# First attention of a gated cross-attention network: the row maxima read from a pair of PSUM banks and a single one

## The chip, the cores and the metric

One Trainium2 chip, one of its cores. The time is the device time of one execution in microseconds (us). Before the change it was 6643.13 us, the median of three runs (6642.96 to 6648.73).

## What is computed

Two layers of gated cross-attention and feed-forward on x of 8 x 256 tokens with 256 features, against a context of 8 x 1601 tokens. The change lies in the attention of the first layer. There the batch is flattened: 2,048 queries meet all 12,808 keys, in 16 heads of 16 features. Queries, keys and values are rounded to 8 bits (fake quantisation), and so are the attention weights, per query:

```
attn = softmax(q @ k.T)                        # (16, 2048, 12808)
s    = max(max(attn, axis=-1) / 255, 1e-8)
attn = clip(round(attn / s), 0, 255) * s
out  = attn @ v
```

Dividing by the row's maximum means that exp(score - max + ln 255) is the number to be rounded, so the kernel needs each query's largest score over all keys before it can take the first exponential of that query.

## The kernel before, in words

`first_attention` works in 32 passes: 16 heads, and for each two chunks of 1,024 queries (`QC`). A pass has `NE` = 102 tiles of 126 keys. `IB` = 4 passes form the body of a loop that runs `LOOPS` = 8 times (the first body is written out before it).

Two computations of the same scores run side by side.

The first is for the exponentials. For tile s PE multiplies keys by queries in two halves of 512 queries (`e_half`, line 1047) into one of two pairs of PSUM banks (banks 0 to 3), with keys on the partitions. ACT takes the exponential of the 126 x 1024 tile into `a_e` (line 1151), POOL rounds it by adding and storing as fp16 in `a_p` (line 918), and PE, four tiles later (`LAG`), multiplies by the values (`av`, line 1087) and adds up the unrounded part for the row sums (line 1091) in bank 4. The scores for exponentials use rows 0 to 53 of PE's array.

The second is for the maxima, one pass ahead. Queries are on the partitions here, and the scores come in `NM` = 201 pieces: 8 tiles of 128 queries x 25 blocks of 512 keys, and one last piece with the 8 keys that are left for each of the 8 query tiles. A piece is one matmul of 512 columns (line 1064) into one of three banks (5, 6, 7), taken in turn (`SLOTS` = 3), and one VectorE reduction by maximum (line 1180) into a column of `a_mx`. These matmuls use rows 64 to 111 of the array. PE waits before piece j until the reduction of piece j - 3 has been counted in `max_done` (line 1062); VectorE waits for `scores_m`. When all 201 pieces of a pass are there, `maximum` reduces the columns (line 1191), and POOL, after rounding tile 93 of the running pass (`SPLIT`), splits the result into three bf16 parts (lines 900 to 910), PE transposes them after tile 98 (`TURN`, line 1073), and ACT copies them into the queries (line 1136), where the next pass's exponentials need them from their tile 0 on.

PE's program is one list, `order`, written before the engines' programs: a half of the scores for exponentials, then a piece of the maxima, then the second half, then a piece, then the values of the tile four back. A pass has 204 such slots for 201 pieces, so three slots are without a piece. The pieces of a pass are rotated: `AHEAD` = 20 of them are made at the end of the pass two before it is used. Waits stand where they are written, and what follows a wait on PE waits with it.

Before the first pass there is an opening: all 201 pieces of pass 0, with nothing else on PE, and then the first `AHEAD` of pass 1.

The DMA queue (SP) loads keys, queries and values of later passes at counts of finished exponentials; its waits do not use the maxima.

Of the kernel before, what the change touches and what calls it, by code (L numbers as in the profile page):

```python
# [9 lines left out]
ALU = mybir.AluOpType  # L10
ACT = mybir.ActivationFunctionType
AX = mybir.AxisListType
# [30 lines left out]
class Shapes:  # L43


    def __init__(self, x_shape, ctx_shape):
        self.B, self.LQ, _ = x_shape
        self.LK = ctx_shape[1]
        self.T = self.B * self.LQ
        self.NT = self.T // P  # L50
        self.NK = self.B * self.LK

        self.QC = 1024
        self.QT = self.QC // P
        self.NC = self.T // self.QC
        self.KT = 126
        self.KTILES = (self.NK + self.KT - 1) // self.KT
        self.NE = self.KTILES
        self.KLAST = self.NK - (self.KTILES - 1) * self.KT
        assert 0 < self.KLAST <= self.KT and self.KTILES % 2 == 0  # L60

        self.SLOTS = 3
        self.WHOLE = self.NK // BANK
        self.LEFT = self.NK - self.WHOLE * BANK
        self.PIECES = [(((t, c * BANK, BANK, 0),), t * (self.WHOLE + 1) + c) for t in range(self.QT) for c in range(self.WHOLE)]
        self.PIECES.append((tuple((t, self.WHOLE * BANK, self.LEFT, t * self.LEFT) for t in range(self.QT)), None))
        self.NM = len(self.PIECES)
        assert 0 < self.LEFT and self.QT * self.LEFT <= BANK and self.NM % self.SLOTS == 0
        self.VQ = (self.KTILES + 3) // 4

        self.KT1 = (self.LK + P - 1) // P
        self.K1LAST = self.LK - (self.KT1 - 1) * P
# [13 lines left out]
class Kernel:  # L86
# [705 lines left out]
    def first_attention(self):  # L792


        nc, sh = self.nc, self.sh
        NE, NM, NC, KT, QC, QT, PIECES = sh.NE, sh.NM, sh.NC, sh.KT, sh.QC, sh.QT, sh.PIECES
        IB = 2 * NC
        LOOPS = HEADS // 2
        RE = 8
        LAG = 4  # L800
        AHEAD = 20
        TURN = NE - 4
        SPLIT = NE - 9
        QW = QC // 4
        V_DMAS = 4
        assert IB == 4 and (IB * NE) % RE == 0 and NE % 2 == 0 and (RE - LAG) >= 2
        LN255 = math.log(255.0)
        K_DMAS, Q_DMAS, O_DMAS = 9, 6, 8
        with ExitStack() as ctx:
# [7 lines left out]
            p = self.sb(ctx, "a_p", [P, RE, QC], F16)  # L817
            sel = self.sb(ctx, "a_sel", [P, 2 * HD])
            mx = self.sb(ctx, "a_mx", [P, QT * (sh.WHOLE + 1)])
# [13 lines left out]
            av_done, scores_m, max_done = (self.sem(ctx, n) for n in ("av_done", "scores_m", "max_done"))  # L833
# [14 lines left out]
            O_BANK, M_BANK = 4, 5  # L848

            def key_rows(t):  # L850
                return sh.KLAST if t == sh.KTILES - 1 else KT

            stream = [("m", 1, j) for j in range(AHEAD, NM)] + [("m", 2, j) for j in range(AHEAD)]
            order, owed = [], []
# [19 lines left out]
            def _(g):  # L876
# [9 lines left out]
                def held(sem, value):  # L886
                    g.wait_ge(sem, value)
                    g.sem_inc(pool_held, 1)

                def split(it, ii, first=False):  # L890

                    n, hb, t0 = it * IB + ii, (ii // NC) % 2, (ii % NC) * QT
                    c = n * LINKS
# [19 lines left out]
                def body(it, i):  # L913
                    for s in range(NE):
                        kk = i * NE + s
                        rows = key_rows(s)
                        held(exp_done, it * (IB * NE) + kk + 1)
                        g.tensor_scalar(p[0:rows, kk % RE, :], e[0:rows, kk % RE, :], 1.0, SHIFT,  # L918
                                        ALU.mult, ALU.add).then_inc(rounded, 1)
                        if s == SPLIT:  # L920
                            held(rounded, it * (IB * NE) + kk + 1)
                            split(it, i + 1)
                split(0, 0, True)
                for i in range(IB):
                    body(0, i)
                with g.Fori(1, LOOPS) as it:
                    for i in range(IB):
                        body(it, i)
# [9 lines left out]
            def load_inv(sp, h, b):  # L938
                sp.dma_start(Kb[M_AT:M_AT + IROWS, b, :], self.d_inv[h]).then_inc(ld_k[b], 16)

            def load_v(sp, h, b, at):
                r = slice(at * P // V_DMAS, (at + 1) * P // V_DMAS)
                sp.dma_start(Vb[r, b, :, :].rearrange("p t d -> p (t d)"), self.d_v0[h, r, 0:sh.KTILES * 2 * HD]).then_inc(ld_v[b], 16)
# [15 lines left out]
            def _(sp):  # L959
# [12 lines left out]
                sp.sem_inc(ld_k[0], 16 * 3)  # L972
                for at in range(V_DMAS):
                    load_v(sp, 0, 0, at)
# [8 lines left out]
                def body(g, i, first):  # L983
# [20 lines left out]
                    if i % NC == 0:  # L1004
# [7 lines left out]
                        load_inv(sp, h, b)  # L1012
                        for at in range(V_DMAS):
                            sp.wait_ge(exp_done, n * NE + 56 + 8 * at)
# [17 lines left out]
                for b in range(2):  # L1032
                    sp.wait_ge(ld_k[b], 16 * K_DMAS * (LOOPS + (b == 0)))
                    sp.wait_ge(ld_v[b], 16 * V_DMAS * (LOOPS + (b == 0)))

            @block.tensor
            def _(pe):
# [14 lines left out]
                def m_piece(g, i, ahead, j, first=False):  # L1052

                    n, ii = g * IB + i + ahead, i + ahead
                    if j == 0:
                        pe.wait_ge(ld_q[ii % 4], 16 * Q_DMAS * (g + ii // 4 + 1))
                        if ii % NC == 0 and not first:
                            pe.wait_ge(ld_k[(ii // NC) % 2], 16 * K_DMAS * (g + ii // NC // 2 + 1))
                    if first and j in range(0, sh.WHOLE, sh.WHOLE // FIRST):
                        pe.wait_ge(ld_first[j // (sh.WHOLE // FIRST)], FIRST_LOADED[j // (sh.WHOLE // FIRST)])  # L1060
                    if not (first and j < sh.SLOTS):
                        pe.wait_ge(max_done, n * NM + j + 1 - sh.SLOTS)
                    for t, k0, wd, c0 in PIECES[j][0]:
                        last = pe.matmul(self.PS[:, M_BANK + j % sh.SLOTS, c0:c0 + wd], Qb[M_ROWS, ii % 4, t * P:(t + 1) * P],  # L1064
                                         Kb[M_ROWS, (ii // NC) % 2, k0:k0 + wd], start=True, stop=True)
                    last.then_inc(scores_m, 1)

                def m_turn(g, i, bank):
                    pe.wait_ge(m_split, g * IB + i + 2)
# [7 lines left out]
                def av(g, i, t, first_ever):  # L1077
# [3 lines left out]
                    if t == 0:  # L1081
                        if not first_ever:
                            pe.wait_ge(gathered, n)
                        if i % NC == 0:
                            pe.wait_ge(ld_v[i // NC], 16 * V_DMAS * (g + 1))
                    for j in range(4):
# [27 lines left out]
                m_turn(0, -1, 2)  # L1114
                for j in range(AHEAD):
                    m_piece(0, 0, 1, j)
# [55 lines left out]

            @block.vector
            def _(v):
                def m_piece(n, j):
                    v.wait_ge(scores_m, n * NM + j + 1)
                    _, col = PIECES[j]
                    bank = self.PS[:, M_BANK + j % sh.SLOTS, :]
                    if col is not None:
                        v.tensor_reduce(mx[:, col:col + 1], bank, AX.X, ALU.max).then_inc(max_done, 1)  # L1180
                    else:
                        dst = mx[:, :].rearrange("p (t c) -> p t c", t=QT)[:, :, sh.WHOLE]
                        v.tensor_reduce(dst, bank[:, 0:QT * sh.LEFT].rearrange("p (t c) -> p t c", t=QT), AX.X,
                                        ALU.max).then_inc(max_done, 1)

                def maximum(n, first):

                    v.wait_ge(max_done, (n + 1) * NM)
                    if not first:
                        v.wait_ge(m_split, n)  # L1190
                    v.tensor_reduce(ms[:, 0, :], mx[:, :].rearrange("p (t c) -> p t c", t=QT), AX.X,
                                    ALU.max).then_inc(m_ready, 1)
                    v.wait_ge(m_ready, n + 1)

                def body(g, i):
                    for j in range(AHEAD, NM):
                        m_piece(g * IB + i + 1, j)
                    maximum(g * IB + i + 1, False)
                    for j in range(AHEAD):
                        m_piece(g * IB + i + 2, j)  # L1200

                for j in range(NM):
                    m_piece(0, j)
                maximum(0, True)
                for j in range(AHEAD):
                    m_piece(1, j)
                for i in range(IB):
                    body(0, i)
                with v.Fori(1, LOOPS) as g:
                    for i in range(IB):  # L1210
                        body(g, i)
# [657 lines left out]
    def second_attention(self):  # L1869
# [11 lines left out]
        SLOTS = 3  # L1881
        AHEAD = 12
        TURN = NE - 2
# [579 lines left out]
```

## Time and profile before

| | |
|---|---|
| median of 3 runs | 6643.13 us |
| profiled execution, its own time | 6652.62 us |
| its span in the profile | 6650.8 us |
| first attention after its opening | 720 to 4900 us |
| PE busy over the span | 5788.3 us (87%) |
| DVE busy | 5609.7 us (84%) |
| ACT busy | 4504.5 us (68%) |
| POOL busy | 3781.9 us (57%) |

PE is TensorE's matmuls and PEld its weight loads, DVE is VectorE, ACT ScalarE, POOL GpSimd, SP the engine that issues the DMAs. Busy time of an engine is the union of its instructions; a group's mean is the length of one instruction, from start to end, and these overlap by a little, so that the distance from start to start is shorter. "Idle before" with an arrow gives the time for which the engine had nothing to do just before such instructions, and whose semaphore ended it. The granted clock is a share of TensorE's full 2.4 GHz; 0.5 is 1.2 GHz. Ends of matmuls are modelled.

### The profile page before, as it was taken

How to read it: one execution, taken by the hardware profiler on the slowest of the kernel's cores; microseconds unless marked ns; L12 is line 12 of the kernel's file. 1: busy time of each engine (PE TensorE's matmuls, PEld its weight loads, DVE VectorE, ACT ScalarE, POOL GpSimd, SP SyncE). 2: the span in 40 equal slices, each digit the busy share in tenths (PEclk: the TensorE clock that was granted, in tenths of full speed). 3: DMA queues.
4: the chain of work that ended last, by engine and by line, in shares of the span. 5: the costliest groups of instructions: out<-in, count | busy, mean ns of one | idle time of the engine just before them, and what ended most of it. 6: DMA issues, size and time to landing. Idle time of an engine off the chain costs nothing. (4 is left out here: it accounts for less than half of the span.)

```text
span 6650.8 us, 180101 instructions
## 1 busy us (share of the span) xinstructions
PE 5788.3 (87%) x64160; PEld 2456.0 (37%) x64160; DVE 5609.7 (84%) x8987; ACT 4504.5 (68%) x4373; POOL 3781.9 (57%) x4001
## 2 busy tenths in 40 slices
PE   2865999999999999999999999999978577999824
PEld 2651233333333333333333333333344353544412
DVE  4877999999999899899989999989963646777786
ACT  0650598898898889888989988988842012666512
POOL 2330488888788788788878878878840001000021
PEclk7995799999999999999999999999989787999966
DMA  1544101101101001011011010010110068777700
GB/s 58 131 115 126 18 9 23 21 8 27 18 11 25 15 16 25 7 24 21 8 27 18 11 25 15 16 23 9 22 37 0 10 267 222 114 110 111 112 28 11
DMA packets 176565, 315.50 MB, mean 47 GB/s; under 512 B 91731, under 2 KB 137812, under 8 KB 171042
## 3 DMA queue, kind: packets, MB, share of 16 engines
q1 hardware_dynamic: 175656, 303.45, 21.3%
q8 instruction: 561, 9.19, 0.6%
q14 instruction: 348, 2.85, 0.2%
HBM read 192.39 MB, written 113.07 MB: 46 GB/s over the span
## 5 line engine op out<-in xcount | busy, mean ns | idle before, releaser
L1180 DVE TENSOR_REDUCE a_mx<-PS 128x1 f32<-128x512 f32 x6620 | 4073.1, 686 | 240.3 <-PE PS L1064 236.7
L1151 ACT ACTIVATE a_e<-PS,a_sk 126x1024 f32<-126x1024 f32 x3264 | 3634.0, 1114 | 494.5 <-PE PS L1047 146.0
L918 POOL TENSOR_SCALAR a_p<-a_e 126x1024 f16<-126x1024 f32 x3264 | 3413.4, 1046 | 681.7 <-ACT a_e L1151 628.6
L1047 PE MATMUL PS<-a_Q,a_K 54*126 54x512 bf16 x6528 | 2112.3, 404 | 31.9 <-issue 22.7
L1064 PE MATMUL PS<-a_K,a_Q 48*128 48x512 bf16 (+1 forms) x6884 | 2108.7, 383 | 31.1 <-POOL a_p L883 30.8
L1091 PE MATMUL PS<-a_e,a_sel 126*32 126x256 f32 x26112 | 1996.2, 382 | 28.1 <-issue 28.1
L1047 PEld LDWEIGHTS PS<-a_Q,a_K 54*126 54x126 bf16 x6528 | 615.3, 131 | 1383.8 <-issue 1325.1
L1087 PE MATMUL PS<-a_p,a_V 128*32 128x256 f16 x13056 | 960.4, 284 | 14.3 <-ACT a_og L1132 10.3
L1087 PEld LDWEIGHTS PS<-a_p,a_V 128*32 128x32 f16 x13056 | 336.8, 93 | 1251.5 <-POOL a_p L918 1053.5
L1091 PEld LDWEIGHTS PS<-a_e,a_sel 126*32 126x32 f32 x26112 | 756.4, 110 | 38.3 <-issue 32.0
L2137 DVE TENSOR_REDUCE b_mx<-PS 128x1 f32<-128x512 f32 x803 | 504.6, 685 | 188.1 <-PE PS L2021 188.0
L2111 ACT ACTIVATE b_e<-PS 128x1024 f32<-128x1024 f32 (+1 forms) x416 | 415.7, 1024 | 223.6 <-PE PS L2041 220.9
L1064 PEld LDWEIGHTS PS<-a_K,a_Q 48*128 48x128 bf16 x6884 | 404.3, 94 | 167.0 <-DVE a_mx L1180 129.4
L2187 POOL TENSOR_SCALAR b_ms<-b_ms 128x8 f32<-128x8 f32 x33 | 7.7, 233 | 631.0 <-DVE b_ms L2148 631.0
L2021 PE MATMUL PS<-b_K,b_Q 96*128 96x512 bf16 (+1 forms) x1070 | 279.8, 346 | 50.1 <-POOL b_K L2172 41.1
L2041 PE MATMUL PS<-b_Q,b_K 99*128 99x256 bf16 (+1 forms) x1664 | 256.0, 277 | 15.4 <-ACT b_e L2111 9.5
L486 PE MATMUL PS<-wkv,cT 128*126 128x256 f32 (+1 forms) x816 | 207.5, 386 | 47.7 <-DVEq L551 47.7
L2056 PE MATMUL PS<-b_e,b_V 128*32 128x256 f32 (+1 forms) x3328 | 229.1, 388 | 9.0 <-ACT b_og L2096 6.6
L1807 POOL MEMSET v1v<- 128x6656 f32 x2 | 11.2, 5646 | 378.8 <-POOLq L1734 378.8
L1846 ACT ACTIVATE k1f<-PS,bk 128x512 f32<-128x512 f32 x64 | 36.3, 593 | 269.5 <-PE PS L1821 269.5
L2041 PEld LDWEIGHTS PS<-b_Q,b_K 99*128 99x128 bf16 (+1 forms) x1664 | 142.2, 99 | 162.2 <-ACT b_e L2111 79.1
L1136 ACT ACTIVATE a_Q<-PS 6x1024 bf16<-6x1024 bf16 x33 | 33.5, 1016 | 242.0 <-PE PS L1073 241.2
(321 smaller groups left out, 3522.1 us busy)
## 6 DMA issues: line engine op xcount, KB each, us to landing
b_K<-d_k SPq DMA_DIRECT2D x210, 200.1 KB, 6.3
a_K<-d_k SPq DMA_DIRECT2D x99, 400.2 KB
d_v<-v1v SPq DMA_DIRECT2D x9, 3328.0 KB, 10.3
b_V<-d_v SPq DMA_DIRECT2D x36, 832.0 KB, 12.4
d_k<-k_T SPq DMA_DIRECT2D x100, 252.0 KB, 4.0
d_k<-k1p SPq DMA_DIRECT2D x54, 400.2 KB, 6.9
a_V<-d_v SPq DMA_DIRECT2D x68, 204.0 KB, 2.8
d_v<-vq SPq DMA_DIRECT2D x17, 803.2 KB
```

The lines of the kernel that those rows point to most:

```text
L918: g.tensor_scalar(p[0:rows, kk % RE, :], e[0:rows, kk % RE, :], 1.0, SHIFT, ALU.mult, ALU.add).then_inc(rounded, 1)
L1047: last = pe.matmul(self.PS[0:key_rows(s), e_bank(i, s) + y, :], Kb[0:E_ROWS, (i // NC) % 2, s * KT:s * KT + key_rows(s)], Qb[0:E_ROWS, i % ...
L1064: last = pe.matmul(self.PS[:, M_BANK + j % sh.SLOTS, c0:c0 + wd], Qb[M_ROWS, ii % 4, t * P:(t + 1) * P], Kb[M_ROWS, (ii // NC) % 2, k0:k0 ...
L1087: pe.matmul(self.PS[32 * j:32 * j + 32, O_BANK, 0:QW], Vb[:, i // NC, t, :], p[:, kk % RE, j * QW:(j + 1) * QW], start=(t == 0), stop=Fals ...
L1091: last = pe.matmul(self.PS[32 * j:32 * j + 32, O_BANK, 0:QW], sel[0:key_rows(t), :], e[0:key_rows(t), kk % RE, j * QW:(j + 1) * QW], start ...
L1151: a.activation(e[0:r, kk % RE, :], self.PS[0:r, e_bank(i, s):e_bank(i, s) + 2, :], ACT.Exp, scale=skb[0:r, hb, s:s + 1]).then_inc(exp_done, 1)
L1180: v.tensor_reduce(mx[:, col:col + 1], bank, AX.X, ALU.max).then_inc(max_done, 1)
L2021: last = pe.matmul(self.PS[:, M_BANK + j % SLOTS, c0:c0 + wd], Qb[0:ROWS, ii % SETS, tq * P:(tq + 1) * P], Kb[0:ROWS, ii % SETS, hh, k0:k0 ...
L2041: last = pe.matmul(self.PS[0:rows, e_bank(s) + j // 2, (j % 2) * LQ:(j % 2 + 1) * LQ], Kb[0:ROWS + MROWS, i % SETS, j, s * P:s * P + rows] ...
L2056: last = pe.matmul(self.PS[32 * j:32 * j + 32, O_BANK, 0:LQ], Vb[0:rows, i // 4, s, i % 4 * QH + j, :], e[0:rows, k % RE, j * LQ:(j + 1) * ...
L2111: a.activation(e[0:r, kk % RE, :], self.PS[0:r, e_bank(s):e_bank(s) + 2, :].rearrange("p b n -> p (b n)"), ACT.Exp).then_inc(exp_done, 1)
L2137: v.tensor_reduce(mx[:, col:col + 1], bank, AX.X, ALU.max).then_inc(max_done, 1)
```

## The change

The three banks are used as a pair and a single one. Pieces 3k and 3k + 1 go to banks 5 and 6, and one reduction reads both (128 x 1024 elements, two results); piece 3k + 2 goes to bank 7 and is reduced alone, as before. A pass then has `NG` = 134 reductions in place of 201. `max_done` and `scores_m` count these groups. PE waits before the first piece of a pair until the pair before has been reduced, before a single piece until the single one before has been, and not at all before the second piece of a pair. It signals VectorE after the second piece of a pair and after a single one. `AHEAD` becomes 21, so that the rotation falls between triples.

```diff
--- before.py
+++ after.py
@@ -66,6 +66,8 @@
         self.PIECES.append((tuple((t, self.WHOLE * BANK, self.LEFT, t * self.LEFT) for t in range(self.QT)), None))
         self.NM = len(self.PIECES)
         assert 0 < self.LEFT and self.QT * self.LEFT <= BANK and self.NM % self.SLOTS == 0
+        self.NG = 2 * (self.NM // self.SLOTS)
+        assert self.SLOTS == 3
         self.VQ = (self.KTILES + 3) // 4
 
         self.KT1 = (self.LK + P - 1) // P
@@ -794,15 +796,18 @@
 
         nc, sh = self.nc, self.sh
         NE, NM, NC, KT, QC, QT, PIECES = sh.NE, sh.NM, sh.NC, sh.KT, sh.QC, sh.QT, sh.PIECES
+        NG = sh.NG
         IB = 2 * NC
         LOOPS = HEADS // 2
         RE = 8
         LAG = 4
-        AHEAD = 20
+        AHEAD = 21
         TURN = NE - 4
         SPLIT = NE - 9
         QW = QC // 4
         V_DMAS = 4
+        group_of = lambda j: 2 * (j // 3) + (j % 3 == 2)
+        assert AHEAD % 3 == 0
         assert IB == 4 and (IB * NE) % RE == 0 and NE % 2 == 0 and (RE - LAG) >= 2
         LN255 = math.log(255.0)
         K_DMAS, Q_DMAS, O_DMAS = 9, 6, 8
@@ -1058,12 +1063,13 @@
                             pe.wait_ge(ld_k[(ii // NC) % 2], 16 * K_DMAS * (g + ii // NC // 2 + 1))
                     if first and j in range(0, sh.WHOLE, sh.WHOLE // FIRST):
                         pe.wait_ge(ld_first[j // (sh.WHOLE // FIRST)], FIRST_LOADED[j // (sh.WHOLE // FIRST)])
-                    if not (first and j < sh.SLOTS):
-                        pe.wait_ge(max_done, n * NM + j + 1 - sh.SLOTS)
+                    if j % 3 != 1 and not (first and j < sh.SLOTS):
+                        pe.wait_ge(max_done, n * NG + group_of(j) - 1)
                     for t, k0, wd, c0 in PIECES[j][0]:
                         last = pe.matmul(self.PS[:, M_BANK + j % sh.SLOTS, c0:c0 + wd], Qb[M_ROWS, ii % 4, t * P:(t + 1) * P],
                                          Kb[M_ROWS, (ii // NC) % 2, k0:k0 + wd], start=True, stop=True)
-                    last.then_inc(scores_m, 1)
+                    if j % 3 != 0:
+                        last.then_inc(scores_m, 1)
 
                 def m_turn(g, i, bank):
                     pe.wait_ge(m_split, g * IB + i + 2)
@@ -1172,20 +1178,28 @@
 
             @block.vector
             def _(v):
-                def m_piece(n, j):
-                    v.wait_ge(scores_m, n * NM + j + 1)
+                def m_group(n, j):
+
+                    v.wait_ge(scores_m, n * NG + group_of(j) + 1)
                     _, col = PIECES[j]
-                    bank = self.PS[:, M_BANK + j % sh.SLOTS, :]
-                    if col is not None:
-                        v.tensor_reduce(mx[:, col:col + 1], bank, AX.X, ALU.max).then_inc(max_done, 1)
+                    if j % 3 == 0:
+                        c1 = PIECES[j + 1][1]
+                        v.tensor_reduce(mx[:, col:c1 + 1:c1 - col], self.PS[:, M_BANK:M_BANK + 2, :], AX.X, ALU.max).then_inc(max_done, 1)
+                    elif col is not None:
+                        v.tensor_reduce(mx[:, col:col + 1], self.PS[:, M_BANK + 2, :], AX.X, ALU.max).then_inc(max_done, 1)
                     else:
                         dst = mx[:, :].rearrange("p (t c) -> p t c", t=QT)[:, :, sh.WHOLE]
-                        v.tensor_reduce(dst, bank[:, 0:QT * sh.LEFT].rearrange("p (t c) -> p t c", t=QT), AX.X,
+                        v.tensor_reduce(dst, self.PS[:, M_BANK + 2, 0:QT * sh.LEFT].rearrange("p (t c) -> p t c", t=QT), AX.X,
                                         ALU.max).then_inc(max_done, 1)
 
+                def m_groups(n, j0, j1):
+                    for j in range(j0, j1):
+                        if j % 3 != 1:
+                            m_group(n, j)
+
                 def maximum(n, first):
 
-                    v.wait_ge(max_done, (n + 1) * NM)
+                    v.wait_ge(max_done, (n + 1) * NG)
                     if not first:
                         v.wait_ge(m_split, n)
                     v.tensor_reduce(ms[:, 0, :], mx[:, :].rearrange("p (t c) -> p t c", t=QT), AX.X,
@@ -1193,17 +1207,13 @@
                     v.wait_ge(m_ready, n + 1)
 
                 def body(g, i):
-                    for j in range(AHEAD, NM):
-                        m_piece(g * IB + i + 1, j)
+                    m_groups(g * IB + i + 1, AHEAD, NM)
                     maximum(g * IB + i + 1, False)
-                    for j in range(AHEAD):
-                        m_piece(g * IB + i + 2, j)
-
-                for j in range(NM):
-                    m_piece(0, j)
+                    m_groups(g * IB + i + 2, 0, AHEAD)
+
+                m_groups(0, 0, NM)
                 maximum(0, True)
-                for j in range(AHEAD):
-                    m_piece(1, j)
+                m_groups(1, 0, AHEAD)
                 for i in range(IB):
                     body(0, i)
                 with v.Fori(1, LOOPS) as g:
```

## Rows read from the trace of the kernel before

**Rows 1.** The page's costliest groups: busy us, mean ns, idle before, releaser.

```profile
L1180 DVE TENSOR_REDUCE a_mx<-PS 128x1 f32<-128x512 f32 x6620 | 4073.1, 686 | 240.3 <-PE PS L1064 236.7
L1151 ACT ACTIVATE a_e<-PS,a_sk 126x1024 f32<-126x1024 f32 x3264 | 3634.0, 1114 | 494.5 <-PE PS L1047 146.0
```

**Rows 2.** Windows: length, busy us of PE, PEld, DVE, ACT, POOL; clock, DMA.

```profile
720.00:4900.00 4180.00, 4106.50 (x52593) 1457.88 (x52592) 3972.42 (x6484) 3673.42 (x3329) 3451.98 (x3454) 0.98 0.09 18
1400.00:1500.00 100.00, 100.00 (x1308) 35.43 (x1296) 98.01 (x161) 90.98 (x82) 84.41 (x86) 1.00 0.01 2
620.00:716.00 96.00, 95.23 (x167) 16.22 (x166) 96.00 (x162) 0.00 (x0) 0.00 (x0) 0.50 0.06 12
5700.00:5800.00 100.00, 96.32 (x958) 50.40 (x952) 78.38 (x138) 68.66 (x73) 5.57 (x25) 1.00 0.82 119
```

**Rows 3.** Timeline in the middle of a pass: start, length, engine.

```profile
2506.81 0.43 PE L1047 MATMUL PS<-a_Q,a_K 54*126 54x512 bf16 x1
2506.82 0.39 PE L1064 MATMUL PS<-a_K,a_Q 48*128 48x512 bf16 x1
...
2508.04 0.43 PE L1047 MATMUL PS<-a_Q,a_K 54*126 54x512 bf16 x1
...
2508.05 0.60 PE L1064 MATMUL PS<-a_K,a_Q 48*128 48x512 bf16 x2
...
2508.51 1.29 DVE L1180 TENSOR_REDUCE a_mx<-PS 128x1 f32<-128x512 f32 x2 [0.54 <-PE PS L1064]
2508.61 0.10 PEld L1087 LDWEIGHTS PS<-a_p,a_V 128*32 128x32 f16 x4 [0.39 <-POOL a_p L918]
...
2509.27 0.43 PE L1047 MATMUL PS<-a_Q,a_K 54*126 54x512 bf16 x1
```

**Rows 4.** Timeline of DVE in one pass and at its boundary.

```profile
2466.75 41.23 DVE L1180 TENSOR_REDUCE a_mx<-PS 128x1 f32<-128x512 f32 x67 [0.54 <-PE PS L1064]
...
2546.49 0.69 DVE L1180 TENSOR_REDUCE a_mx<-PS 128x1 f32<-128x512 f32 x1 [0.43 <-PE PS L1064]
2547.51 3.13 DVE L1180 TENSOR_REDUCE a_mx<-PS 128x1 f32<-128x512 f32 x5 [0.33 <-PE PS L1064]
2551.18 8.60 DVE L1180 TENSOR_REDUCE a_mx<-PS 128x1 f32<-128x512 f32 x14 [0.54 <-PE PS L1064]
```

**Rows 5.** Timeline of the opening, before any exponential: DVE and PE's loads.

```profile
679.45 10.84 DVE L1180 TENSOR_REDUCE a_mx<-PS 128x1 f32<-128x512 f32 x18
...
680.05 0.68 DVE L1180 TENSOR_REDUCE a_mx<-PS 128x1 f32<-128x512 f32 x1
...
680.78 0.10 PEld L1064 LDWEIGHTS PS<-a_K,a_Q 48*128 48x128 bf16 x1 [0.49 <-DVE a_mx L1180]
```

**Rows 6.** Groups by line from 720 to 4900 us: idle time and its releaser.

```profile
L1180 DVE TENSOR_REDUCE a_mx<-PS 128x1 f32<-128x512 f32 x6420 | 3953.4, 686 | 209.6 <-PE PS L1064 206.0
L1151 ACT ACTIVATE a_e<-PS,a_sk 126x1024 f32<-126x1024 f32 x3232 | 3598.5, 1114 | 491.4 <-PE PS L1047 146.0
L918 POOL TENSOR_SCALAR a_p<-a_e 126x1024 f16<-126x1024 f32 x3231 | 3379.0, 1046 | 679.1 <-ACT a_e L1151 628.6 <-POOL a_mparts L910 11.0
...
L1064 PEld LDWEIGHTS PS<-a_K,a_Q 48*128 48x128 bf16 x6676 | 383.9, 94 | 37.0 <-DVE a_mx L1180 32.8 <-issue 0.5
```

**Rows 7.** DVE's groups that take 1,024 elements, later in the program.

```profile
L2375 DVE SCALAR_TENSOR_TENSOR gt<-PS,fst,gb 128x1024 f32<-128x1024 f32 x16 | 20.5, 1284 | 28.6 <-PE PS L2314 28.6
L2385 DVE TENSOR_REDUCE gs<-gt 128x1 f32<-128x1024 f32 x16 | 19.5, 1220 | 0.6
```

**Rows 8.** Timeline of a tile at the lower clock.

```profile
1766.88 0.68 PE L1047 MATMUL PS<-a_Q,a_K 54*126 54x512 bf16 x1
...
1766.88 1.03 PE L1064 MATMUL PS<-a_K,a_Q 48*128 48x512 bf16 x2
...
1767.60 1.29 DVE L1180 TENSOR_REDUCE a_mx<-PS 128x1 f32<-128x512 f32 x2 [6.03 <-PE PS L1064]
...
1769.10 0.69 PE L1047 MATMUL PS<-a_Q,a_K 54*126 54x512 bf16 x1
```

## The prediction

> **What bounds the kernel now.** I read the page's groups first. The maxima are the costliest group, 6,620 reductions of 512 scores, and 3,264 exponentials say how many tiles there are: 32 passes of 102 [rows 1]. The windows come next. From 720 to 4900 us, the first attention after its opening, PE is busy 98% of the time and DVE 95% at a mean granted clock of 0.98; at 1400 to 1500 us they are at 100% and 98% [rows 2]. Two engines look full, so the shares don't decide. The timeline does. Tiles follow each other every 1.23 us on PE (2506.81, 2508.04, 2509.27), and PE's part needs no wait: scores from 2508.04, V products from 2508.61 (0.57 later), the next scores 0.66 after that [rows 3]. At 2506.82 a tile has one score block for the maxima in place of two, and it takes the same 1.23 us. DVE, left without a block there, idles 0.54 us, released by PE, and restarts at 2508.51 with no backlog [rows 3]. Between two such holes it makes 67 reductions in 41.23 us, (41.23 - 0.68)/66 = 0.614 us apart, just PE's pace of half a tile [rows 4]. At the opening, where nothing but DVE sets the pace, they stand (10.84 - 0.68)/17 = 0.598 apart [rows 5]. So PE sets the tile and DVE follows, with 2 x (0.614 - 0.598) = 0.03 us per tile to spare. In the whole stage PE's loads waited for DVE 32.8 us in sum; DVE waited for PE 206.0 us [rows 6].
>
> **The change, part by part.** Pieces come in triples. Of three reductions two become one over 1,024 elements. What a long one takes: 1.22 us for a reduction of 1,024 from SBUF, and 1.28 us for another operation that reads 1,024 from PSUM [rows 7]. One of 512 from PSUM takes 0.68 [rows 5]. I take 1.22, which is the same operation; 1.28 is kept as the upper end, and 0.68, no dearer than a short one, belongs to a rival below. DVE's starts then fall from 3 x 0.598 = 1.79 to (1.22 - 0.08) + 0.598 = 1.74 us per triple: 0.05 us that nobody waits for.
>
> The other part is the buffering, and it costs. Before, PE may write a piece as soon as the one three back is read: up to two are in hand while DVE reads. Now the first piece of a pair waits until the whole pair before it has been read, and DVE starts the pair when its second piece is written. The pair's two banks are filled or read, never both; only the single bank works beside them. The wait stands in PE's program before the late scores, the V products and the next tile, so all of these queue behind it.
>
> One turn of the pair, in steps:
> - filling it when both pieces lie in one tile: 0.60 us for two [rows 3];
> - filling it when it straddles two tiles: the piece that waited ends 0.39 after the wait opens (one block, 2506.82). V products start 0.04 before such an end (2508.61 against 2508.05 + 0.60), so at 0.35; the next tile's scores 0.66 later, and their block 0.39 more: 1.40 us [rows 3];
> - to DVE's start: 2508.51 - (2508.05 + 0.39) = 0.07 us [rows 3];
> - the read: 1.22 us [rows 7];
> - back to PE: a reduction that starts at 680.05 ends at 680.73, and the load that waits for it starts at 680.78: 0.05 us [rows 5].
>
> Turns are 0.60 + 1.34 = 1.94 and 1.40 + 1.34 = 2.74 us. A triple is a tile and a half, so the two kinds alternate; both make 4.68 us for three tiles that now take 3.69: 0.99 us more. The tile goes from 1.23 to 1.56 us on average. A pass has 67 triples, 33.5 couples x 0.99 = 33.2 us. Off this I take 1.5 us: the three slots without a piece and PE's own pauses around the pass boundary (DVE idles there 0.43, 0.33, 0.54 us [rows 4]) let a pair drain unseen. 32 passes x 31.7 = 1,014 us.
>
> Two corrections. With the clock at 1.2 GHz a tile already takes 2.22 us (1766.88 to 1769.10) and two blocks 1.03 [rows 8]; a pair's turn is then 1.03 + 1.34 = 2.37 us, and it hides in the tile and a half of 3.3. A mean of 0.98 [rows 2] puts (1 - 0.98)/(1 - 0.50) = 4% of the stage at that clock, 167 us; I count 130 us of it, the rest being pauses, as 60 tiles that lose nothing: 60 x 0.33 = -20 us. At the opening, 620 to 716 us, the clock is 0.50 [rows 2], only these blocks run, and DVE's own three reads make a triple 1.79 us. The pair's turn of 2.37 replaces it: 74 triples (67, and 7 of the next pass) x 0.58 = +43 us.
>
> The rest moves nothing. One wait less per triple on PE and one increment less are in no gap of the trace. AHEAD of 21 for 20 keeps a triple whole and brings the last piece of a pass one slot, 0.6 us, earlier. The softmax chain behind the maximum (the splitting on POOL at tile 93, the transposes) gets five slower tiles to hide in, so it brings no loss. ACT (1.11 of 1.23 us) and POOL (1.05) [rows 6] have more time per tile than now. SP's loads hang on the tiles' count and come later with them. The second attention isn't touched.
>
> **Sum.** 1,014 - 20 + 43 = +1,037 us on the profiled execution, 6652.6 us by itself (span 6650.8 and 1.8 around it). This stands 9.5 us above the median of 6643.1, so I predict 6643 + 1,037, rounded to 7,680 us.
>
> **Two rules beside the rows.** The Trainium skill, Perfetto Trace Analysis, section "Optimizing Scalar/DVE Operations", says that larger operations can improve throughput if the engine is saturated, and also that an engine which isn't saturated but leaves bubbles on others may do better with its instructions broken up. By the first the kernel would gain the 0.05 us per triple; by the second it loses. DVE's 0.54 us idle without a backlog makes the second the one that applies here, and no run here has shown its size.
>
> **Rivals.**
> *DVE is the bound, the kernel gets faster.* For it: DVE is busy 98% at 1400 us [rows 2], and its 0.614 per piece is near its 0.598. If the shared idle were an artefact, the pace would be the reductions', and 33 passes x 67 x 0.05 to 0.06 = 110 to 135 us would go: 6,520 us. It decides where filling the pair and both hand-overs fit into the single read beside it: 0.60 us against 0.60 + 0.12 and 1.40 + 0.12. Neither fits. Chance 0.03.
> *A read of two banks takes hardly longer than one.* Were it 0.68 us, the turns would be 1.40 and 2.20, in sum 3.60 under 3.69, and the tile would stay at PE's 1.23: 6,645 us. Against it stand the rows of 1.22 and 1.28 us for 1,024 elements [rows 7]. It decides below some 0.73 us. Chance 0.04.
> *The clock falls.* PE now stands still for 0.3 of each 1.56 us. In this stage the lower clock comes with long pauses (6.03 us at DVE before the tiles of [rows 8]), and at 620 to 716 us it stays there although a block is issued every 0.60 us [rows 2]; at 5700 to 5800 PE has small pauses and the clock is 1.00 [rows 2]. If it stayed at 1.2 GHz, tiles would take 2.22 us [rows 8]: 3,264 x 0.99 = +3,230, or 9,870 us; if it did so a third of the time, near 8,400. PE would still do most of its present work per us, far more than at the opening, and this is what I hold against it. Chance 0.08.
> The Trainium skill has such a rule: TensorE: Matmul & The Clock Gate, section "A second HAM failure mode: psum-queue depth-cycling", tells of a kernel whose micro-idles between groups of matmuls made the clock swing between its two levels. No row of this trace shows it for pauses as short as these.
>
> **How the numbers follow.** Forecast 0.85. Its own range: hand-over of 0.04 in place of 0.07, more turns absorbed, or part of the late scores overlapping the wait takes off up to 230 us; reading at 1.28 adds 2 x 0.06 x 33.5 x 32 = 129 us, and some passes at the lower clock add up to 150 more. That gives 7,450 to 7,950, and the rivals, all outside it, with what these bounds may miss leave some 2 in 10 out. This kernel's measurements tell 0.2% (13 us) from no change. Faster: 0.03. Within 0.2%: 0.04. Slower: 0.93, the forecast, the clock and what lies between.
>
> **What would show it.** Right: tiles alternating between 1.23 us and about 1.7 us with a mean near 1.56; PE's loads at the maxima's line waiting for DVE in about two tiles of three, and some 1,000 us of such waits in sum where there were 32.8; reductions of 2 x 512 at 1.22 us; DVE's share falling to some 75 to 80%; the clock still near 0.98. Wrong: tiles of 1.23 us with DVE as idle as before (the pair fits after all), a pair read far from 1.22, or a granted clock well under 0.9 in the stage.

## The result, and the profile after

The changed kernel takes 7607.8 us (median of 4 runs, 7600.64 to 7615.57) against 6645.9 us of the kernel before in the same comparison: a ratio of 1.1447, 95% interval 1.1427 to 1.1466, +962 us. The forecast was 7,680 us in a range of 7,450 to 7,950. The profiled execution took 7600.6 us, with a span of 7598.8 us.

In the changed kernel's rows L1052 is the scores for the exponentials, L1069 the blocks for the maxima, L1093 and L1097 the products with the values and the row sums, L1157 the exponential, L1187 the wide reduction and L1189 the single one. The page's groups, with the columns of [rows 1]:

```profile
L1157 ACT ACTIVATE a_e<-PS,a_sk 126x1024 f32<-126x1024 f32 x3264 | 3633.9, 1114 | 1403.5 <-PE PS L1052 1388.8
...
L1187 DVE TENSOR_REDUCE a_mx<-PS 128x2 f32<-128x1024 f32 x2218 | 2717.4, 1225 | 1198.4 <-PE PS L1069 1097.0
...
L1189 DVE TENSOR_REDUCE a_mx<-PS 128x1 f32<-128x512 f32 x2185 | 1488.3, 681 | 43.3 <-PE PS L1069 43.3
...
L1069 PEld LDWEIGHTS PS<-a_K,a_Q 48*128 48x128 bf16 x6885 | 464.7, 94 | 1161.0 <-DVE a_mx L1187 1076.6
```

Two reductions in three have become one of 1,225 ns. DVE is idle 1,097 us before the wide ones, released by PE, and the loads of the blocks for the maxima (PEld) are idle 1,077 us, released by the wide reduction. Each waits for the other in turn. These are sums over the whole execution, opening included; before the change they were 237 us [rows 1] and, for the loads, 129 us. In the passes alone, from 760 to 5800 us:

```profile
L1187 DVE TENSOR_REDUCE a_mx<-PS 128x2 f32<-128x1024 f32 x2127 | 2606.0, 1225 | 1116.3 <-PE PS L1069 1015.9
...
L1069 PEld LDWEIGHTS PS<-a_K,a_Q 48*128 48x128 bf16 x6599 | 443.9, 94 | 980.0 <-DVE a_mx L1187 959.4 <-DVE a_mx L1189 13.9 <-issue 1.8
```

That is 1,016 and 959 us, where [rows 6] had 206 and 33. ACT's work is unchanged at 3,634 us, and its idle time before it has gone from 494 us [rows 1] to 1,404.

The windows, with the columns of [rows 2]:

```profile
720.00:5900.00 5180.00, 4884.98 (x52798) 1641.54 (x52798) 3970.62 (x4393) 3682.47 (x3333) 3460.37 (x3462) 0.99 0.08 15
1400.00:1500.00 100.00, 95.59 (x1046) 31.84 (x1043) 77.08 (x86) 73.42 (x67) 69.14 (x67) 1.00 0.19 31
620.00:716.00 96.00, 59.48 (x123) 9.22 (x121) 74.31 (x83) 0.00 (x0) 0.00 (x0) 0.50 0.06 12
```

The engine that looked nearly full (95% and 98%) is now at 77%, and PE at 94 to 96%. PE still reads as busy because a matmul's span is longer than the distance to the next (0.38 us, and 0.60 for two in a row), and these spans bridge most of a pause: its share does not show that it stands still. The clock is at 0.99, no lower than before.

The timeline in the middle of a pass shows the turns. Columns as in [rows 3].

```profile
3101.17 0.09 PEld L1069 LDWEIGHTS PS<-a_K,a_Q 48*128 48x128 bf16 x1 [0.55 <-DVE a_mx L1187]
...
3101.49 0.10 PEld L1093 LDWEIGHTS PS<-a_p,a_V 128*32 128x32 f16 x4 [0.23 <-issue]
...
3102.15 0.60 PE L1069 MATMUL PS<-a_K,a_Q 48*128 48x512 bf16 x2
...
3102.62 1.23 DVE L1187 TENSOR_REDUCE a_mx<-PS 128x2 f32<-128x1024 f32 x1 [0.90 <-PE PS L1069]
3102.72 0.10 PEld L1093 LDWEIGHTS PS<-a_p,a_V 128*32 128x32 f16 x4 [0.39 <-issue]
...
3103.38 0.43 PE L1052 MATMUL PS<-a_Q,a_K 54*126 54x512 bf16 x1
...
3103.90 0.09 PEld L1069 LDWEIGHTS PS<-a_K,a_Q 48*128 48x128 bf16 x1 [0.40 <-DVE a_mx L1187]
...
3104.13 0.38 PE L1069 MATMUL PS<-a_K,a_Q 48*128 48x512 bf16 x1
...
3104.54 1.23 DVE L1187 TENSOR_REDUCE a_mx<-PS 128x2 f32<-128x1024 f32 x1
...
3105.09 0.43 PE L1052 MATMUL PS<-a_Q,a_K 54*126 54x512 bf16 x1
...
3105.82 0.09 PEld L1069 LDWEIGHTS PS<-a_K,a_Q 48*128 48x128 bf16 x1 [0.55 <-DVE a_mx L1187]
```

At 3101.17 the wait for the pair opens, in the second half of a tile; the V products follow at 3101.49, the next tile's blocks at 3102.15, and the wide read starts at 3102.62. It ends at 3103.85, and at 3103.90 the loads for the next pair start: this turn took 2.73 us. That next pair lies in one tile: its blocks at 3103.90 and 3104.13, the read at 3104.54 (ending 3105.77), the next loads at 3105.82, a turn of 1.92 us. The first half of the scores (3103.38, 3105.09) goes out before the wait; the second half, the V products and the next tile stand behind it.

A pass is the distance between two reductions of all maxima's columns (line 1191 before, 1205 after). Before:

```profile
2537.09 0.37 DVE L1191 TENSOR_REDUCE a_ms<-a_mx 128x8 f32<-128x208 f32 x1
...
2664.51 0.37 DVE L1191 TENSOR_REDUCE a_ms<-a_mx 128x8 f32<-128x208 f32 x1
```

After:

```profile
3131.90 0.37 DVE L1205 TENSOR_REDUCE a_ms<-a_mx 128x8 f32<-128x208 f32 x1
...
3288.87 0.37 DVE L1205 TENSOR_REDUCE a_ms<-a_mx 128x8 f32<-128x208 f32 x1
```

127.42 us have become 156.97: a regular pass takes 29.55 us more. All 32 passes lie between the first and the last of these reductions, before and after:

```profile
L1191 DVE TENSOR_REDUCE a_ms<-a_mx x33: 369/370/370, 716.2 to 4886.1; 128x8 f32<-128x208 f32 x33
```

```profile
L1205 DVE TENSOR_REDUCE a_ms<-a_mx x33: 369/369/370, 753.8 to 5838.1; 128x8 f32<-128x208 f32 x33
```

4,169.9 us have become 5,084.3, so the passes together lost 914 us, 28.6 each on average. Not all are regular: six took 139 to 142 us before, one in every four, where the loop's body starts again, and these lost 21 to 28 us. The opening shows in the first scores for exponentials, before

```profile
730.97 0.69 PE L1047 MATMUL PS<-a_Q,a_K 54*126 54x512 bf16 x1
```

and after:

```profile
772.38 0.68 PE L1052 MATMUL PS<-a_Q,a_K 54*126 54x512 bf16 x1
```

That is 41.4 us later; the first reduction of all columns is 37.6 us later (716.2 and 753.8). Together 37.6 + 914.4 = 952 us, and what follows the last of these reductions took 1,764.7 us before and 1,760.7 after, which gives the 948 us between the two profiled spans.

### The profile page after: what moved, and what is told of

It reads as the page before. It is cut to its first block and busy times, and to the rows that moved or that the text cites. A ratio compares the mean times of both kernels' runs of the same rounds, so it can differ in the third digit from the quotient of the medians.

```text
span 7598.8 us, 174133 instructions
## 1 busy us (share of the span) xinstructions
PE 6499.7 (86%) x64161; PEld 2612.3 (34%) x64161; DVE 5563.4 (73%) x6770; ACT 4507.9 (59%) x4373; POOL 3786.6 (50%) x4001
## 5 line engine op out<-in xcount | busy, mean ns | idle before, releaser
L1157 ACT ACTIVATE a_e<-PS,a_sk 126x1024 f32<-126x1024 f32 x3264 | 3633.9, 1114 | 1403.5 <-PE PS L1052 1388.8
L1187 DVE TENSOR_REDUCE a_mx<-PS 128x2 f32<-128x1024 f32 x2218 | 2717.4, 1225 | 1198.4 <-PE PS L1069 1097.0
L1069 PE MATMUL PS<-a_K,a_Q 48*128 48x512 bf16 (+1 forms) x6885 | 2234.1, 384 | 299.6 <-DVE a_mx L1187 80.3
L1052 PE MATMUL PS<-a_Q,a_K 54*126 54x512 bf16 x6528 | 2324.4, 411 | 21.9 <-issue 17.3
L1097 PE MATMUL PS<-a_e,a_sel 126*32 126x256 f32 x26112 | 1986.4, 381 | 25.1 <-issue 25.1
L1189 DVE TENSOR_REDUCE a_mx<-PS 128x1 f32<-128x512 f32 x2185 | 1488.3, 681 | 43.3 <-PE PS L1069 43.3
L1052 PEld LDWEIGHTS PS<-a_Q,a_K 54*126 54x126 bf16 x6528 | 683.0, 130 | 1354.5 <-issue 1313.4
L1093 PE MATMUL PS<-a_p,a_V 128*32 128x256 f16 x13056 | 956.9, 283 | 0.9
L1069 PEld LDWEIGHTS PS<-a_K,a_Q 48*128 48x128 bf16 x6885 | 464.7, 94 | 1161.0 <-DVE a_mx L1187 1076.6
L1097 PEld LDWEIGHTS PS<-a_e,a_sel 126*32 126x32 f32 x26112 | 753.2, 110 | 33.9 <-issue 26.6
L1093 PEld LDWEIGHTS PS<-a_p,a_V 128*32 128x32 f16 x13056 | 335.3, 93 | 1091.0 <-issue 1004.9
L2121 ACT ACTIVATE b_e<-PS 128x1024 f32<-128x1024 f32 (+1 forms) x416 | 415.7, 1024 | 221.9 <-PE PS L2051 219.1
L2031 PE MATMUL PS<-b_K,b_Q 96*128 96x512 bf16 (+1 forms) x1070 | 279.6, 347 | 48.5 <-POOL b_K L2182 41.4
L1142 ACT ACTIVATE a_Q<-PS 6x1024 bf16<-6x1024 bf16 x33 | 33.5, 1015 | 279.2 <-PE PS L1079 278.5
```

Source lines behind the costliest of these rows:

```text
L1052: last = pe.matmul(self.PS[0:key_rows(s), e_bank(i, s) + y, :], Kb[0:E_ROWS, (i // NC) % 2, s * KT:s * KT + key_rows(s)], Qb[0:E_ROWS, i % ...
L1093: pe.matmul(self.PS[32 * j:32 * j + 32, O_BANK, 0:QW], Vb[:, i // NC, t, :], p[:, kk % RE, j * QW:(j + 1) * QW], start=(t == 0), stop=Fals ...
L1097: last = pe.matmul(self.PS[32 * j:32 * j + 32, O_BANK, 0:QW], sel[0:key_rows(t), :], e[0:key_rows(t), kk % RE, j * QW:(j + 1) * QW], start ...
L1157: a.activation(e[0:r, kk % RE, :], self.PS[0:r, e_bank(i, s):e_bank(i, s) + 2, :], ACT.Exp, scale=skb[0:r, hb, s:s + 1]).then_inc(exp_done, 1)
L1187: v.tensor_reduce(mx[:, col:c1 + 1:c1 - col], self.PS[:, M_BANK:M_BANK + 2, :], AX.X, ALU.max).then_inc(max_done, 1)
L1189: v.tensor_reduce(mx[:, col:col + 1], self.PS[:, M_BANK + 2, :], AX.X, ALU.max).then_inc(max_done, 1)
```

## The experiments

The theory of the **turn**: a pair of banks is filled or read, never both; its turn (fill, hand-over, read, hand-over) is longer than the tile and a half in which PE wants it back, and PE's program queues behind the wait. Rivals: the **wide read** as such costs; the **bookkeeping** does (semaphores, the rotation); or **where** the wait stands decides and the read's length does not. Every ratio is to the kernel before on the same chip.

### The pair read by two short reductions

```diff
-  v.tensor_reduce(mx[:, col:c1 + 1:c1 - col], self.PS[:, M_BANK:M_BANK + 2, :], ...)
+  v.tensor_reduce(mx[:, col:col + 1], self.PS[:, M_BANK, :], ...)
+  v.tensor_reduce(mx[:, c1:c1 + 1], self.PS[:, M_BANK + 1, :], ...)
```

`max_done` counts pieces again, with the waits at the same places.

> The changed kernel with its waits, its order and its filling of the pair kept, but the pair read by two reductions of 512, one for each bank, begun when both are written; PE still waits for the second. Theory of the turn (the pair's two banks are filled or read, never both, and PE's program queues behind the wait): the read of the pair becomes 0.60 + 0.68 = 1.28 us in place of 1.225, 0.055 us more for each of 67 x 32 turns, so about 7,730 us. Rival of the wide read (one instruction over two banks is itself what costs, by holding PSUM or DVE): without it the time falls back near the kernel before, 6,650 to 6,800 us. Rival of the bookkeeping (the pair's semaphores): it would not move, 7,608.

Measured: 7751.7 us, ratio 1.1663 (1.1643 to 1.1682). The loads behind the wait, in the timeline:

```profile
3000.51 0.09 PEld L1069 LDWEIGHTS PS<-a_K,a_Q 48*128 48x128 bf16 x1 [0.46 <-DVE a_mx L1188]
...
3002.50 0.09 PEld L1069 LDWEIGHTS PS<-a_K,a_Q 48*128 48x128 bf16 x1 [0.61 <-DVE a_mx L1188]
...
3005.29 0.09 PEld L1069 LDWEIGHTS PS<-a_K,a_Q 48*128 48x128 bf16 x1 [0.46 <-DVE a_mx L1188]
```

Turns of 1.99 and 2.79 us, 0.07 and 0.06 longer than the change's, where 0.055 was expected. Some 0.065 us on each of 67 x 32 turns is 139 us, most of the 144 by which the time grew; 7,730 us was expected, 22 less than measured. No instruction reads two banks here, and the loss is larger. The wide read is not the cause; it is the better way of reading under this wait.

### The wide reduction over half, and over three quarters, of its columns

```diff
-  v.tensor_reduce(mx[:, col:c1 + 1:c1 - col], self.PS[:, M_BANK:M_BANK + 2, :], ...)
+  v.tensor_reduce(mx[:, col:c1 + 1:c1 - col], self.PS[:, M_BANK:M_BANK + 2, 0:256], ...)
```

and the same with `0:384`. In both, `LN255` is lowered by 12 as well, which the cut leaves out.

> The changed kernel, with the wide reduction taking 256 columns of each of its two banks (half of the scores of two pieces in three are left out of the maxima, and the exponent's offset is lowered by 12 so that nothing overflows). Theory of the turn: the read falls from 1.225 to about 0.68 us, the turns from 1.92 and 2.73 to 1.38 and 2.19, in sum 3.57 under the 3.69 us of three tiles, so the tile is back at 1.23 us and the kernel near 6,650 us (6,630 to 6,720). Rival of the straddle alone (what costs is where the wait stands in PE's program, not how long the read is): it stays above 7,300. Rival of the wide read over two banks as such: stays near 7,600.

> The changed kernel with the wide reduction taking 384 columns of each bank (a quarter of the scores of two pieces in three left out; offset of the exponent lowered by 12). Theory of the turn: the read is 1.225 - 256/0.96 GHz-like share, that is half way between 0.68 and 1.225, 0.95 us; turns of 1.65 and 2.46, in sum 4.11 against 3.69: 0.42 us for three tiles, 33.5 x 32 x 0.42 = 450, less about 90 absorbed, plus some 25 in the opening: about 7,030 us (6,930 to 7,120). A cost that goes with the number of wide reads and not with their length would give the 7,608 of the change.

Measured: 6636.1 us, ratio 0.9986 (0.9976 to 0.9995), and 7080.2 us, ratio 1.0646 (1.0629 to 1.0664). Groups of the first from 2000 to 3000 us, with the columns of [rows 6]:

```profile
L1187 DVE TENSOR_REDUCE a_mx<-PS 128x2 f32<-128x512 f32 x513 | 355.0, 692 | 213.9 <-PE PS L1069 213.9
L1189 DVE TENSOR_REDUCE a_mx<-PS 128x1 f32<-128x512 f32 x506 | 347.3, 686 | 101.7 <-PE PS L1069 101.7
...
L1069 PEld LDWEIGHTS PS<-a_K,a_Q 48*128 48x128 bf16 x1595 | 106.1, 94 | 14.9 <-DVE a_mx L1189 3.3
```

and of the second:

```profile
L1187 DVE TENSOR_REDUCE a_mx<-PS 128x2 f32<-128x768 f32 x472 | 452.3, 958 | 213.7 <-PE PS L1069 191.8
```

With a read of 692 ns the loads wait for no pair any more, though the semaphores, the order and the straddling are those of the change: bookkeeping and place alone cost nothing. Loss against length of the read: none at 0.69 us, 434 us at 0.96, 962 at 1.225. From the point where the turns fit (0.73 us by the prediction's rival) the first step costs 434/228 = 1.9 us for each ns of read and the second 528/267 = 2.0; one turn for each of 67 x 32 triples would give 2.1. Three lengths lie on one straight line with a threshold, as a turn gives; the threshold itself is the prediction's, not a measured point. Why the first ends 10 us below the kernel before, just outside its interval, is left open.

### No pair across two tiles

```diff
                     order.append(stream[at])
                     at += 1
+                    if y == 1 and stream[at - 1][2] % 3 == 0:
+                        order.append(stream[at])
+                        at += 1
```

> The changed kernel with one edit in PE's list: where a pair would begin in the second half of a tile, its second piece is made right behind the first instead of in the next tile, so that no pair straddles two tiles. Theory of the turn: every fill is about 0.60 us and a turn 1.94, but pairs are then needed every 1.23 + 0.2 us and 2.4 us by turns; the short distance costs 0.7 us per three tiles in place of 0.96, so the tile is about 1.46 us, less what is absorbed at the pass boundary: about 7,350 us (7,250 to 7,450). Rival of the wide read: where the matmuls stand does not matter, 7,600.

Measured: 7400.8 us, ratio 1.1137 (1.1119 to 1.1156). In its timeline a pair's blocks, its read, and the next pair's:

```profile
3002.16 0.60 PE L1072 MATMUL PS<-a_K,a_Q 48*128 48x512 bf16 x2
...
3002.87 1.23 DVE L1190 TENSOR_REDUCE a_mx<-PS 128x2 f32<-128x1024 f32 x1 [0.46 <-PE PS L1072]
...
3004.15 0.11 PEld L1072 LDWEIGHTS PS<-a_K,a_Q 48*128 48x128 bf16 x2 [0.58 <-DVE a_mx L1190]
3004.15 0.60 PE L1072 MATMUL PS<-a_K,a_Q 48*128 48x512 bf16 x2
...
3004.79 1.23 DVE L1190 TENSOR_REDUCE a_mx<-PS 128x2 f32<-128x1024 f32 x1
```

The turn is 1.99 us (3002.16 to 3004.15), 0.05 more than expected, no straddle is left, and 207 us have come back. The rest stays: filling and reading one after the other takes longer than the distance to the next pair whichever way the pieces are laid. So the straddle is a part of the loss, about a fifth. That the rest is the lack of a second buffer for the pair follows from the length of the turn and from the short reads above; no run gave the pair a second buffer.

### Two slots in place of three, no pairs

```diff
-        self.SLOTS = 3
+        self.SLOTS = 2
```

with the slot chosen by (pass + piece) mod 2, since a pass has an odd number of pieces (those lines are left out here).

> The kernel before with two slots of one bank in place of three, every piece reduced alone as before. Theory of the turn: a bank is used again two pieces, one tile, later; the second bank of a tile is written at 0.60 us, read from about 1.06 to 1.74 because DVE has the other first, and free at 1.79, where PE wants it at 1.23 + 0.2: PE waits about 0.35 us in every second tile. Tile about 1.39 us, less what is absorbed, and some 20 us in the opening: about 7,120 us (6,950 to 7,200). Rival of the wide read: without a wide read nothing is lost, 6,646 us.

Measured: 7155.2 us, ratio 1.0772 (1.0754 to 1.0790).

```profile
3000.04 0.43 PE L1047 MATMUL PS<-a_Q,a_K 54*126 54x512 bf16 x1
...
3000.63 0.09 PEld L1064 LDWEIGHTS PS<-a_K,a_Q 48*128 48x128 bf16 x1 [0.40 <-DVE a_mx L1180]
...
3001.60 0.43 PE L1047 MATMUL PS<-a_Q,a_K 54*126 54x512 bf16 x1
...
3002.83 0.43 PE L1047 MATMUL PS<-a_Q,a_K 54*126 54x512 bf16 x1
```

Tiles of 1.56 and 1.23 us by turns, 1.395 on average for the 1.39 expected, with the load at 3000.63 held for 0.40 us by a reduction. The kernel before needs its third slot, though with it PE's loads hardly wait for DVE (32.8 us in the stage [rows 6]): taking it away costs 509 us without any change in the reads. The change loses more, since two of its three banks open and close together.

### The kernel before with reads of 256 columns, and with AHEAD at 21

```diff
-  v.tensor_reduce(mx[:, col:col + 1], bank, AX.X, ALU.max).then_inc(max_done, 1)
+  v.tensor_reduce(mx[:, col:col + 1], bank[:, 0:256], AX.X, ALU.max).then_inc(max_done, 1)
```

> The kernel before with every maximum taken over 256 of its 512 columns (half of the scores are left out of the maxima; offset of the exponent lowered by 12). Theory that PE sets the tile: DVE's work falls by some 0.27 us per piece and the tile stays at 1.228 us; only the opening, where DVE sets the pace, gains: there the piece falls from 0.598 to PE's 0.43 us, 208 x 0.17 = -35 us, so about 6,610 us. Rival that DVE is the bound (or half of it): the tile falls well below 1.23, to 1.19 or less (ACT), 6,500 us or less.

Here too `LN255` is lowered by 12. Measured: 6614.6 us, ratio 0.9949 (0.9933 to 0.9966), 31 us less.

```profile
L1180 DVE TENSOR_REDUCE a_mx<-PS 128x1 f32<-128x256 f32 x1531 | 581.7, 420 | 410.2 <-PE PS L1064 409.0
```

```profile
L1191 DVE TENSOR_REDUCE a_ms<-a_mx x33: 369/370/370, 682.1 to 4844.8; 128x8 f32<-128x208 f32 x33
```

From 2000 to 3000 us a reduction takes 420 ns in place of 686 and DVE stands idle 410 us. The opening ends 34 us earlier (682.1 for 716.2); the 32 passes take 4,162.7 us where they took 4,169.9, so nearly all of the gain is the opening's. The 0.05 us per triple that the wide read saves could not have been worth anything in a pass.

```diff
-        AHEAD = 20
+        AHEAD = 21
```

> The kernel before with AHEAD at 21 in place of 20, the only part of the change that can be made alone: one piece more of a pass is made a pass earlier. Theory of the turn: nothing to lose or gain, 6,646 us within 5. Rival: the rotation moves the end of the maxima against POOL's chain and is part of the loss, over 6,700.

Measured: 6649.5 us, ratio 1.0004 (0.9995 to 1.0014). The rotation costs nothing.

### The kernel before with the values made for two tiles at a time

```diff
-                order += owed
-                owed = []
+                if y == 1 and s % 2 == 1:
+                    order += owed
+                    owed = []
```

> The kernel before with the products with the values made for two tiles together behind every second tile, so that PE changes half as often between the scores (rows 0 to 111 of the array) and the values (all rows, four column groups). Theory that PE's own sequence of 1.228 us paces the tile, some 0.2 us of it being the two changes: up to 0.1 us per tile could go, until ACT and DVE bound it at about 1.19 to 1.20 us: 3,264 x 0.03 = -100, 6,545 us. It could also lose: two tiles of scores in a row find only two pairs of banks, and the second waits for ACT. If the pauses are not PE's own, no change or a loss, up to 6,900.

Measured: 7027.7 us, ratio 1.0573 (1.0555 to 1.0590): slower than the 6,900 at which the expectation ended, and not by the wait for ACT that it named. From 2000 to 3000 us the loads for the maxima wait 193.1 us for DVE, and the loads of scores for exponentials 30.1 us for ACT.

```profile
2400.00 0.43 PE L1048 MATMUL PS<-a_Q,a_K 54*126 54x512 bf16 x1
...
2400.01 0.60 PE L1065 MATMUL PS<-a_K,a_Q 48*128 48x512 bf16 x2
...
2400.47 2.48 DVE L1181 TENSOR_REDUCE a_mx<-PS 128x1 f32<-128x512 f32 x4 [0.25 <-PE PS L1065]
...
2401.22 0.09 PEld L1065 LDWEIGHTS PS<-a_K,a_Q 48*128 48x128 bf16 x1 [0.60 <-DVE a_mx L1181]
...
2402.74 0.43 PE L1048 MATMUL PS<-a_Q,a_K 54*126 54x512 bf16 x1
```

Two tiles take 2.74 us (2400.00 to 2402.74). Four blocks for the maxima now come in a row, and the fourth, at 2401.22, is held 0.60 us by the reduction that must free its bank: with three slots and a read of 0.68 us a burst of four doesn't fit. It is again a turn, that of a single bank. Whether PE with fewer changes between scores and values would be faster where the slots allow it stays open.

None of these is faster than the kernel before with the whole computation in it.

## Why the prediction was right

**What bounds the kernel.** PE's sequence and not DVE's 98%: the run with short reads left the passes within 7 us of 4,170 and gained 31 us, where 35 were expected, nearly all in the opening. POOL could be thought a third bound, since the page of the kernel before puts most of the waits of the values' loads down to it; the changed kernel's page does not:

```profile
L1087 PEld LDWEIGHTS PS<-a_p,a_V 128*32 128x32 f16 x13056 | 336.8, 93 | 1251.5 <-POOL a_p L918 1053.5
```

```profile
L1093 PEld LDWEIGHTS PS<-a_p,a_V 128*32 128x32 f16 x13056 | 335.3, 93 | 1091.0 <-issue 1004.9
```

A tile of the changed kernel that waits for no pair (3102.15 to 3103.38 in the timeline above) still takes 1.23 us, with its values' loads 0.57 us behind the scores and the next scores 0.66 us behind those, just as before, though ACT, POOL and DVE all have idle time there. So these gaps are PE's own, and neither POOL nor ACT set the tile.

**The sizes of a turn.** Forecast 1.94 and 2.74 us, measured 1.92 and 2.73; the read 1.22, measured 1.225, although the row it came from reads SBUF and this one PSUM. That part was a choice between two rows that came out well: the other, 1.28, would have added 129 us. Tiles are 1.23 us and about 1.7, as forecast, and in two of three a load waits; they do not alternate, though, but come as two long ones to each short one. The loads' waits for the wide reduction came out at 959 us in the passes, for "some 1,000", and DVE's share at 77%, for 75 to 80.

**The sum.** Forecast +1,037, measured +962 in the medians and +948 between the two profiled executions. The opening was taken at +43 us and measured 41.4 up to the first scores for exponentials: a pair's turn there is 2.35 us, from read to read,

```profile
691.29 1.22 DVE L1187 TENSOR_REDUCE a_mx<-PS 128x2 f32<-128x1024 f32 x1 [0.53 <-PE PS L1069]
692.44 0.68 DVE L1189 TENSOR_REDUCE a_mx<-PS 128x1 f32<-128x512 f32 x1
692.57 0.13 PEld L1069 LDWEIGHTS PS<-a_K,a_Q 48*128 48x128 bf16 x2 [1.66 <-DVE a_mx L1187]
...
693.64 1.23 DVE L1187 TENSOR_REDUCE a_mx<-PS 128x2 f32<-128x1024 f32 x1 [0.53 <-PE PS L1069]
```

for 2.37. What was mis-sized most is the term of 1.5 us per pass for turns that drain unseen. The couples give 33.5 x (4.65 - 3.69) = 32.2 us, one less than the 33.2 written; a regular pass lost 29.5 (29.55 for the two quoted), so 2.7 us were absorbed. That this happens at the slots without a piece and at the pauses of the pass boundary is argued, and no run separates it. Over 32 passes the two differences make (31.7 - 29.5) x 32 = 70 of the 89 us between 1,037 and 948. The term of -20 us for tiles at the lower clock was small as well: 32 regular passes would have lost 944 us and the real ones lost 914, 30 us less, in passes that were longer before. That is 10 more of the 89; how much of the 30 is the clock's is not separated. The last 9 are 5 in the opening up to the first maximum (37.6 for 43) and 4 behind the last pass.

**The clock.** The rival did not come: the mean granted clock is 0.99 over the stage, with PE's loads for the maxima held 0.40 to 0.55 us in two tiles of three. The Trainium skill tells of a kernel whose clock swung between its levels with micro-idles (TensorE: Matmul & The Clock Gate, "A second HAM failure mode: psum-queue depth-cycling"). This trace does not show that for pauses of half a microsecond: 0.98 before, 0.99 after.

**The two other rivals.** DVE as the bound fell with the short reads. A wide read hardly longer than a short one would indeed have cost nothing: made artificially 0.69 us long it gives the time of before. The rival's condition was right and its premise was not.

## What to carry to other kernels

A slot that several instructions fill and one reads is free only when all of it has been read: write down its turn (fill, signal, read, signal) and compare it with the distance at which the producer comes back, before counting what a merged instruction saves. Where an engine takes its program in the order written, as PE did at these waits, the wait also stops everything that is written behind it, so a fill that straddles a long piece of other work counts that work into the turn. An engine that is 98% busy need not be the bound: look whether it restarts without a backlog after a hole in its work.

## What the runs showed that was not expected

Merging the two reads is itself worth 144 us (7751.7 against 7607.8) once the pair's wait is there, where merging saves nothing without it: the same 0.06 us or so per turn is free in one kernel and on the path in the other. And a burst of four blocks into three slots cost 382 us, more than the 100 us that the expectation hoped to gain by fewer changes between scores and values.
